# Moving the next batch's column norms and its query-weight product ahead of the output projection, in a two-layer post-norm kernel with five engines

## The chip, the cores and the metric

The kernel runs on one core of one Trainium2 chip. The metric is the device time of one execution in microseconds (us), the median of several runs. One further execution was recorded by the hardware profiler; all views of the profile and of the trace below belong to that one.

## What is computed

The input is 8 batches of 1024 tokens with 256 features. Two layers follow each other, each an attention-like step and a feed-forward step, and after each of the four steps the input is added back and a layer norm over the 256 features is taken. Cut to what matters here:

```python
# step 1: linear attention. Q, K, V = x @ W.T + b; Q and K are divided by their norms over the tokens
inv = 1.0 / jnp.linalg.norm(t, ord=2, axis=-2)
tailor_sum = 1.0 / (L + einsum('bnc,bc->bn', Q, sum(K, -1) + EPS))
matrix = einsum('bmn,bcn->bmc', K, V)
out = x + gamma * (value_sum + einsum('bnm,bmc->bcn', Q, matrix)) * tailor_sum
# step 2: 8 experts, all computed for every token, weighted with a thresholded softmax of x @ gate_w
# step 3: attention between the 16 heads of one token, then the output projection
out = einsum('bni,mi->bnm', attn @ v, Wproj) + bproj
# step 4: the best 768 of each 1024 tokens by a router score are replaced by gelu(x @ w_block)
```

The norms of step 1 are over tokens, so the kernel first makes the Gram matrix of a batch, multiplies it with the weights of Q and K, and gets the squared norms of all columns and the product with the query weights from that. These last two, called NORM and G, are what the change moves. The output projection of step 3 is called PR.

## The kernel before

**Stages.** The batches pass through a software pipeline written out by hand. In `turn(a, b, c)` batch a goes through step 1, batch b = a - 1 through step 2 and the projections to q, k and v, and batch c = a - 2 through steps 3 and 4. Turns are named by a here: turn 0 and turn 1 lack c (and b), turns 2 to 7 are full, then `closing` and `ending` finish the last two batches. Each engine has its own `turn` function, a fixed list of steps; an engine works its list strictly in order, and a step that waits for a semaphore holds everything behind it. So the written order is the schedule.

**Names.** `a_...` steps belong to batch a (also the expert steps `a_moe(b, t)`, t = 0 to 7, one for each 128 tokens; `ln(b, 4..7, 0)` is the norm after them), `b_...` steps to batch c (steps 3 and 4) or b. `TP` is 4: pairs of 128-token tiles. PSUM has eight banks: two for `a_` results, two for `b_` results, used in turn by the order of `A_USES` and `B_USES`, and four for the experts.

**Around the change**, in a full turn:

- TensorE (`pe`): `a_moe(b, 4)` (24 matmuls of 512 columns), `b_pr(c, 0..3)` (PR: 56 matmuls of 256 columns; it waits for `o_loaded`, the attention output of batch c, which is written to memory and read back in another layout by DMA: `scratch_o<-stage`, then `bt<-scratch_o`), `a_norm(a)` (NORM, 4 small fp32 matmuls, which show as 8 records; it waits for `t_sum`, from GpSimd), `a_g(a)` (G, fp32, 256 columns), `a_moe(b, 5)`, then `b_tz(c, 0..3)`, transposes of batch c's normalised rows `x3`.
- VectorE (`dve`): `a_moe(b, 4)`, `b_pr(c, p)` (add PR to `x3` at L1517, statistics at L1294 and L1299), `a_norm(a)` (copy the norms out of PSUM, L1326), `a_moe(b, 5)`, `b_tz(c, 0)` and `b_tz(c, 1)` (the low half of the split copy `ct`), `a_g(a)`.
- GpSimd (`pool`): `a_tsum(a)` (L632, L635, gives `t_sum`), `a_sum(b, 4)` (L619, L622, L626: adds ScalarE's expert parts), `ln(c, 0..3, 1)` (1/sqrt of the variance after PR), `a_norm(a)` (power -0.5 of the norms, L639).
- ScalarE (`act`), which the change doesn't touch: `a_moe(b, 4)`, `a_ln2n(b, 1)`, `b_prn(c, 0..3)` (normalises the rows after PR, L915, waits for `ln(c, p, 1)`), `a_moe(b, 5)` (four scaled copies out of expert banks 2 and 3, `part<-bank`), `b_tz(c, 0..3)` (the high half of `ct`, L794).

Two lines matter more than the others, since each stands at the head of a step that holds its engine:

```python
act.wait_ge(b_rs, 8 * b + p + 1)          # b_prn: ScalarE, ahead of its a_moe(b, 5)
pool.wait_ge(a_free[a_ring("NORM")], a_read(a, "NORM"))   # a_norm: GpSimd, waits for VectorE's copy
```

Of the kernel before, what the change touches and what calls it, by code (L numbers as in the profile page):

```python
# [5 lines left out]
def build_two_layer_postln(nc, x, wqk_t, bqk, wv, bv, gamma, gate_w, gate_b, expert_w, expert_b,  # L6
# [38 lines left out]
    with ctx:  # L45
# [200 lines left out]
        def a_ring(name):  # L246
            return a_use(name) % 2
# [14 lines left out]
        def a_read(a, name):  # L262
            return a * (UA // 2) + a_use(name) // 2 + 2
# [313 lines left out]
        def _(pool):  # L577
# [38 lines left out]
            def a_sum(a, t):  # L616

                pool.wait_ge(parted, T * a + t + 1)
                pool.tensor_tensor(part[:, 0:2, :], part[:, 0:2, :], part[:, 2:4, :], ALU.add)\  # L619
                    .then_inc(part_sum, 1)  # L620
                pool.wait_ge(part_sum, 2 * T * a + 2 * t + 1)
                pool.tensor_tensor(part[:, 0, :], part[:, 0, :], part[:, 1, :], ALU.add)\  # L622
                    .then_inc(part_sum, 1)
                pool.wait_ge(part_sum, 2 * T * a + 2 * t + 2)
                pool.wait_ge(chained, T * a + t + 1)
                pool.tensor_tensor(x1[:, t, :], x1[:, t, :], part[:, 0, :], ALU.add)\  # L626
                    .then_inc(moe_ready, 1)

            def a_tsum(a):
                pool.wait_ge(t_prod, 2 * a + 2)  # L630
                pool.sem_inc(waits_held, 1)
                pool.tensor_tensor(prod[:, 0, :], prod[:, 0, :], prod[:, 1, :], ALU.add).then_inc(t_sum, 1)  # L632
                pool.wait_ge(t_sum, 2 * a + 1)
                pool.wait_ge(t_row, a + 1)
                pool.tensor_tensor(prod[0:1, 0, :], prod[0:1, 0, :], prow, ALU.add).then_inc(t_sum, 1)  # L635

            def a_norm(a):
                pool.wait_ge(a_free[a_ring("NORM")], a_read(a, "NORM"))
                pool.tensor_tensor(inv[:, :], nrm[:, :], half[:, 0:4], ALU.pow).then_inc(inv_ready, 1)  # L639
# [29 lines left out]
            def turn(a, b, c):  # L669
                if b is not None:  # L670
                    a_sum(b, 0)
                    if c is not None:
                        b_turnv(c, 0)
                    a_sum(b, 1)
                if c is not None:
                    b_s(c, 0)
                    b_s(c, 1)
                    b_turnv(c, 1)
                if b is not None:
                    a_sum(b, 2)  # L680
                    ln(b, 4, 0)
                if c is not None:
                    b_s(c, 2)
                    b_s(c, 3)
                if b is not None:
                    a_sum(b, 3)
                    ln(b, 5, 0)
                if a is not None:
                    a_tsum(a)
                if b is not None:  # L690
                    a_sum(b, 4)
                if c is not None:
                    ln(c, 0, 1)
                    ln(c, 1, 1)
                    ln(c, 2, 1)
                    ln(c, 3, 1)
                if a is not None:
                    a_norm(a)
                if b is not None:
                    a_sum(b, 5)  # L700
                    ln(b, 6, 0)
                    a_sum(b, 6)
                    a_sum(b, 7)
                if c is not None:
                    ln(c, 4, 1)
                if b is not None:
                    ln(b, 7, 0)
                if c is not None:
                    ln(c, 5, 1)
                    b_store(c, 0)  # L710
                if a is not None:
                    ln(a, 0, 0)
                if c is not None:
                    b_store(c, 1)
                if b is not None:
                    b_copy(b, 0)
                if a is not None:
                    ln(a, 1, 0)
                if c is not None:
                    ln(c, 6, 1)  # L720
                if b is not None:
                    b_copy(b, 1)
                if c is not None:
                    ln(c, 7, 1)
                    b_store(c, 2)
                    b_store(c, 3)
                if b is not None:
                    b_copy(b, 2)
                if a is not None:
                    ln(a, 2, 0)  # L730
                if b is not None:
                    b_copy(b, 3)
                if a is not None:
                    ln(a, 3, 0)
                    if a + 1 < NB:
                        for p in range(TP):
                            a_xs(a + 1, p)
# [523 lines left out]
        def _(dve):  # L1261
# [62 lines left out]
            def a_norm(a):  # L1324
                dve.wait_ge(a_full, a_filled(a, "NORM"))
                dve.tensor_copy(nrm[:, :], a_ps("NORM")[:, 0:4]).then_inc(a_free[a_ring("NORM")], 1)  # L1326
# [100 lines left out]
            def a_moe(a, t):  # L1427
                dst = x1[:, t, :]
                if t % 2 == 0:
                    dve.wait_ge(a_free[a_ring(f"BIAS{t // 2}")], a_read(a, f"BIAS{t // 2}"))  # L1430
                for e in range(4):
                    q = e // 2
                    if e % 2 == 0:
                        dve.wait_ge(m_full, 32 * a + 4 * t + q + 1)
                    ins = dve.scalar_tensor_tensor(out=dst, in0=m_bank[q][:, D * (e % 2):D * (e % 2 + 1)],  # L1435
                                                   scalar=wexp[:, t, e:e + 1], in1=dst, op0=ALU.mult,
                                                   op1=ALU.add)
                    if e % 2 == 0:
                        ins.then_inc(m_step, 1)
                        dve.wait_ge(m_step, 2 * T * a + 2 * t + q + 1)  # L1440
                    else:
                        ins.then_inc(m_free[q], 1)
                        if q == 0:
                            dve.wait_ge(m_free[q], T * a + t + 2)
                dve.wait_ge(m_free[1], T * a + t + 2)
                dve.sem_inc(chained, 1)
# [152 lines left out]
            def turn(a, b, c):  # L1599
# [34 lines left out]
                    split_weights(range(0, 1))  # L1634
                if b is not None:
                    a_moe(b, 4)
                if c is not None:
                    for p in range(TP):
                        b_pr(c, p)
                if a is not None:  # L1640
                    a_norm(a)
                if b is not None:
                    a_moe(b, 5)
                if c is not None:
# [203 lines left out]
        def _(pe):  # L1848
# [49 lines left out]
            def a_norm(a):  # L1898
                pe.wait_ge(a_free[a_ring("NORM")], a_before(a, "NORM"))
                pe.wait_ge(t_sum, 2 * a + 2)  # L1900
                for c in range(4):
                    ins = pe.matmul(a_ps("NORM")[:, c:c + 1], prod[:, 0, P * c:P * (c + 1)], ones[:, 0:1],
                                    start=True, stop=True)
                ins.then_inc(a_full, 1)

            def a_g(a):
                pe.wait_ge(t_row, a + 1)
                pe.wait_ge(a_free[a_ring("G")], a_before(a, "G"))
                for m in range(KD):
                    cols = slice(D + P * m, D + P * (m + 1))  # L1910
                    ins = sum_of(a_ps("G")[:, D * m:D * (m + 1)],
                                 [(wqk[:, k, cols], tq[:, k, 0:D]) for k in range(KD)]
                                 + [(brow[0:1, cols], trow[0:1, 0:D])])
                ins.then_inc(a_full, 1)
# [63 lines left out]
            def a_moe(a, t, qs=range(4)):  # L1978
                for q in qs:
                    if t == 0 and later(a):  # L1980
                        pe.wait_ge(ff_read, 4 * (a - 1) + q + 1)
                    pe.wait_ge(m_free[q], T * a + t + 1)
                    sum_of(m_bank[q][:, :], split_terms(lambda k, i: at[:, k, i, tok(t)],
                                                        lambda k, j: we[:, j, k, 512 * q:512 * (q + 1)]))\
                        .then_inc(m_full, 1)
# [107 lines left out]
            def turn(a, b, c):  # L2093
# [31 lines left out]
                    a_tx(a, 1)  # L2125
                if b is not None:
                    a_moe(b, 4)
                if c is not None:
                    b_pr(c, 0)
                    b_pr(c, 1)  # L2130
                    b_pr(c, 2)
                    b_pr(c, 3)
                if a is not None:
                    a_norm(a)
                    a_g(a)
                if b is not None:
                    a_moe(b, 5)
                if c is not None:
# [220 lines left out]
```

## Time and profile before

| | us |
|---|---|
| median of 3 runs | 1359.78 (1359.39 to 1360.84) |
| profiled execution | 1357.91 |
| its span, first to last instruction | 1356.1 |
| mean granted TensorE clock, share of full speed | 0.886 |
| TensorE busy | 1167.6 (86%) |
| VectorE busy | 939.6 (69%) |
| ScalarE busy | 723.5 (53%) |
| GpSimd busy | 575.4 (42%) |

The profile's names are PE (TensorE matmuls), PEld (its weight loads), DVE (VectorE), ACT (ScalarE), POOL (GpSimd), SPq (the queue that issues most DMAs). A busy share is a mean over stages that have different limits, so what a change in one stage is worth must be read from the chain of waits in that stage. The profiled execution is 1.9 us below the median of the runs.

### The profile page before, as it was taken

The numbers are of one execution on the slowest core, as the hardware profiler recorded it, in microseconds if no ns is written. First come the engines' busy times: TensorE is split into PE (matmuls) and PEld (weight loads), VectorE is DVE, ScalarE is ACT, GpSimd is POOL, SyncE is SP. The second block draws the span as 40 slices with busy tenths as digits, with TensorE's granted clock in tenths as the row PEclk, the third lists the DMA queues.
The fourth block names the chain that finished last, engine by engine and source line by source line (L and its number), as shares of the span: only waits on it lengthen the run. The fifth ranks groups of instructions, "written<-read, shape, count | busy, mean of one in ns | idle before, by whom it ended". The sixth has DMA issues, their size and how long they took to land.

```text
span 1356.1 us, 31150 instructions
## 1 busy us (share of the span) xinstructions
PE 1167.6 (86%) x12264; PEld 749.5 (55%) x12264; DVE 939.6 (69%) x2118; ACT 723.5 (53%) x1152; POOL 575.4 (42%) x880
## 2 busy tenths in 40 slices
PE   6688899998989899998999989998999888996643
PEld 4444456655665546655665646555566555653532
DVE  3544578676766868677775868668776877656854
ACT  3223375347753575547853576447853566544444
POOL 2235335435354356345354355245354254350333
PEclk8789898799979997899979999799988998698566
DMA  5000092204802084202902065201902066108221
GB/s 187 16 1 16 31 154 21 80 9 113 114 3 78 19 173 44 79 9 92 135 2 79 17 164 56 56 24 61 170 6 64 1 138 81 38 27 156 33 79 47
DMA packets 93145, 90.64 MB, mean 67 GB/s; under 512 B 7110, under 2 KB 81864, under 8 KB 92744
## 3 DMA queue, kind: packets, MB, share of 16 engines
q1 hardware_dynamic: 80648, 75.54, 29.7%
q0 software_dynamic: 2560, 8.39, 1.8%
q10 hardware_dynamic: 9792, 4.72, 1.5%
q8 instruction: 98, 1.61, 0.5%
q14 instruction: 47, 0.39, 0.1%
HBM read 46.68 MB, written 41.94 MB: 65 GB/s over the span
## 4 chain that ended last, share of the span: by engine, by line
PE 55%; DVE 18%; DMA 6%; ACT 6%; issue 6%; POOL 6%; SPq 1%; ACTq 1%; POOLq 0%; DVEq 0%
PE bank L1852 52%; DVE keys L1546 2%; POOL rs L604 2%; DMA bt<-scratch_o 2%; DVE x L1435 2%; DVE stats L1294 2%; DVE gelu L1548 2%; DMA scratch_o<-stage 2%; PE bank L1862 2%; ACT x L915 1%; DVE ct L1263 1%; DVE gt L1349 1%; DVE x L1575 1%; ACT part L794 1%; ACT stage L794 1%
## 5 line engine op out<-in xcount | busy, mean ns | idle before, releaser
L1852 PE MATMUL bank<-we,at 128*128 128x512 f16 x1536 | 370.9, 400 | 1.9 <-DVE x L1435 1.9
L1852 PEld LDWEIGHTS bank<-we,at 128*128 128x128 f16 x1536 | 153.9, 102 | 192.4 <-issue 38.4
L619 POOL TENSOR_TENSOR part<-part 128x512 f32<-128x512 f32 x64 | 84.2, 1315 | 272.6 <-ACTq L941 272.6
L794 ACT ACTIVATE part<-bank,wexp 128x256 f32<-128x256 f32 x256 | 104.7, 472 | 160.3 <-PE bank L1852 99.7
L1435 DVE SCALAR_TENSOR_TENSOR x<-bank,wexp,x 128x256 f32<-128x256 f32 x256 | 122.7, 479 | 53.2 <-PE bank L1852 46.7
L1852 PE MATMUL bank<-bt,wqkv 128*128 128x512 f16 x576 | 137.1, 380 | 18.3 <-DVE stage L1263 12.3
L915 ACT ACTIVATE x<-x,nm,rs 128x256 f32<-128x256 f32 x192 | 104.5, 593 | 81.5 <-POOL nm L607 80.2
L1263 DVE TENSOR_TENSOR stage<-bank,stage 128x512 f16<-128x512 f32 x112 | 75.7, 686 | 86.5 <-ACT stage L794 86.2
L600 POOL TENSOR_SCALAR nm<-mv 128x2 f32<-128x2 f32 x128 | 33.6, 262 | 219.6 <-DVE mv L1299 213.9
L1852 PE MATMUL bank<-keys,blockdiag 128*128 128x16 f16 x3072 | 97.2, 193 | 22.1 <-DMA keys<-scratch_qkv 11.9
L1852 PEld LDWEIGHTS bank<-keys,blockdiag 128*128 128x128 f16 x3072 | 95.8, 103 | 26.9 <-issue 12.9
L794 ACT ACTIVATE stage<-bank 128x512 f16<-128x512 f32 x112 | 66.0, 597 | 80.0 <-PE bank L1852 74.5
L604 POOL TENSOR_TENSOR rs<-ve,half 128x2 f32<-128x2 f32 x128 | 96.0, 750 | 10.7
L1852 PEld LDWEIGHTS bank<-bt,wqkv 128*128 128x128 f16 x576 | 52.2, 98 | 83.8 <-DVE stage L1263 22.6
L1862 PE MATMUL bank<-const,x 128*128 128x128 f32 x384 | 59.8, 285 | 38.4 <-ACT x L915 24.0
L1852 PE MATMUL bank<-xs,blockdiag 128*128 128x16 f16 x2688 | 72.8, 172 | 16.9 <-issue 16.7
L1852 PEld LDWEIGHTS bank<-xs,blockdiag 128*128 128x128 f16 x2688 | 71.7, 101 | 19.0 <-issue 18.7
L794 ACT ACTIVATE blockdiag<-stage,const 128x2048 f16<-128x2048 f16 x40 | 78.1, 1994 | 1.5 <-DVE stage L1478 1.5
L1294 DVE BATCH_NORM_STATS2 stats<-x 128x6 f32<-128x256 f32 x192 | 71.9, 416 | 7.8 <-POOL x L626 4.1
L654 POOL COPY stage<-ct 128x2048 f16<-128x2048 f16 x14 | 53.3, 3810 | 56.2 <-DMA ct<-scratch_qkv 56.2
L1862 PEld LDWEIGHTS bank<-const,x 128*128 128x128 f32 x384 | 45.9, 146 | 53.9 <-ACT x L915 31.1
L1462 DVE TENSOR_SCALAR blockdiag<-stage,const 128x2048 f16<-128x2048 f16 x88 | 74.9, 902 | 0.0
(197 smaller groups left out, 2239.6 us busy)
## 6 DMA issues: line engine op xcount, KB each, us to landing
scratch_qkv<-stage SPq DMA_DIRECT2D x40, 512.0 KB, 3.5
ct<-scratch_qkv SPq DMA_DIRECT2D x112, 128.0 KB, 6.8
x_in<-in_x_dram SPq DMA_DIRECT2D x32, 256.0 KB, 2.8
keys<-scratch_qkv SPq DMA_DIRECT2D x64, 128.0 KB, 6.1
bt<-scratch_o SPq DMA_DIRECT2D x16, 512.0 KB, 4.1
out_dram<-x POOLq DMA_DIRECT2D x32, 256.0 KB, 2.6
scratch_qkv<-part SPq DMA_DIRECT2D x8, 512.0 KB, 8.1
scratch_o<-stage SPq DMA_DIRECT2D x32, 128.0 KB, 3.5
```

The source lines that it names most:

```text
L600: pool.tensor_scalar(nm[side][:, k, :], mv[side][:, k, :, 0], -1.0, None, ALU.mult)
L604: pool.tensor_tensor(rs[side][:, k, :], ve[side][:, k, :], half[:, 0:2], ALU.pow)\
L619: pool.tensor_tensor(part[:, 0:2, :], part[:, 0:2, :], part[:, 2:4, :], ALU.add)\
L654: pool.tensor_copy(v_rows[hf].rearrange("p (s c) h -> p s c h", c=8), turned(v_home(b), hf)).then_inc(v_turned[hf], 1)
L794: return act.activation(dst, src, ACT.Copy, scale=scale)
L915: ins = act.activation(dsts[t], srcs[t], ACT.Identity, bias=nm[side][:, k, t:t + 1], scale=rs[side][:, k, t:t + 1])
L1263: return dve.tensor_tensor(dst, src, hi, ALU.subtract)
L1294: ins = dve.bn_stats(stats[side][:, t, :], srcs[t])
L1435: ins = dve.scalar_tensor_tensor(out=dst, in0=m_bank[q][:, D * (e % 2):D * (e % 2 + 1)], scalar=wexp[:, t, e:e + 1], in1=dst, op0=ALU.mult ...
L1462: ins = dve.tensor_scalar(blockdiag[:, dst_half, :, DH * r:DH * (r + 1)], rows, mask[:, r:r + 1], None, ALU.mult)
L1852: ins = pe.matmul(dst, lhs, rhs, start=(n == 0), stop=(n == len(terms) - 1))
L1862: ins = pe.transpose(ps[:, 2 * P * k + P * t:2 * P * k + P * (t + 1)], src[:, 2 * p + t, P * k:P * (k + 1)], ident)
```

## The change

On TensorE `a_norm(a)` and `a_g(a)` go from behind the four `b_pr(c, p)` to ahead of them, right behind `a_moe(b, 4)`. On VectorE `a_norm(a)` goes ahead of `b_pr(c, p)`; `a_g(a)` stays. On GpSimd `a_norm(a)` goes ahead of `a_sum(b, 4)` and `ln(c, 0..3, 1)`, right behind `a_tsum(a)`. ScalarE and the DMA queues keep their lists. The order of use of the PSUM banks stays. Turns 2 to 7 change on all three engines, turn 1 on GpSimd alone.

```diff
@@ GpSimd, turn
                 if a is not None:
                     a_tsum(a)
+                if a is not None:
+                    a_norm(a)
                 if b is not None:
                     a_sum(b, 4)
                 if c is not None:
...
                     ln(c, 3, 1)
-                if a is not None:
-                    a_norm(a)
@@ VectorE, turn
                 if b is not None:
                     a_moe(b, 4)
+                if a is not None:
+                    a_norm(a)
                 if c is not None:
                     for p in range(TP):
                         b_pr(c, p)
-                if a is not None:
-                    a_norm(a)
@@ TensorE, turn
                 if b is not None:
                     a_moe(b, 4)
+                if a is not None:
+                    a_norm(a)
+                    a_g(a)
                 if c is not None:
                     b_pr(c, 0)
                     b_pr(c, 1)
                     b_pr(c, 2)
                     b_pr(c, 3)
-                if a is not None:
-                    a_norm(a)
-                    a_g(a)
```

TensorE in turn 2, before. `we` is the expert weight (so x24 is one `a_moe`), `wproj` and `bproj` are PR, `ones,shared` is NORM, `wqk` and `brow` are G:

```order
L1852 MATMUL bank<-we,at 128x512 x24
L1852 MATMUL bank<-wproj,bt 128x256 x6
L1852 MATMUL bank<-bproj,rows 128x256
...
L1902 MATMUL bank<-ones,shared 128x1 x4
L1852 MATMUL bank<-xs,wqk 128x256 x2
L1852 MATMUL bank<-xs,brow 128x256
...
L1852 MATMUL bank<-we,at 128x512 x24
L1862 MATMUL bank<-const,x 128x128 x16
```

And with the change:

```order
L1852 MATMUL bank<-we,at 128x512 x24
L1902 MATMUL bank<-ones,shared 128x1 x4
L1852 MATMUL bank<-xs,wqk 128x256 x2
L1852 MATMUL bank<-xs,brow 128x256
...
L1852 MATMUL bank<-wproj,bt 128x256 x6
L1852 MATMUL bank<-bproj,rows 128x256
...
L1852 MATMUL bank<-we,at 128x512 x24
L1862 MATMUL bank<-const,x 128x128 x16
```

NORM and G now stand between one expert step and PR; PR stands directly ahead of the next expert step. What follows, the transposes (`const,x`), is where it was.

GpSimd in turn 2, before. `shared` is `a_tsum`, `part` and `x` are `a_sum`, `nm`, `ve`, `rs` one `ln`, `inv` is `a_norm`:

```order
L632 TENSOR_TENSOR shared<-shared 128x512
L635 TENSOR_TENSOR shared<-shared,xs 1x512
L619 TENSOR_TENSOR part<-part 128x512
...
L626 TENSOR_TENSOR x<-x,part 128x256
L600 TENSOR_SCALAR nm<-mv 128x2
...
L607 TENSOR_TENSOR nm<-nm,rs 128x2
L639 TENSOR_TENSOR inv<-nrm,half 128x4
```

And with the change:

```order
L632 TENSOR_TENSOR shared<-shared 128x512
L635 TENSOR_TENSOR shared<-shared,xs 1x512
L639 TENSOR_TENSOR inv<-nrm,half 128x4
L619 TENSOR_TENSOR part<-part 128x512
...
L626 TENSOR_TENSOR x<-x,part 128x256
L600 TENSOR_SCALAR nm<-mv 128x2
...
L607 TENSOR_TENSOR nm<-nm,rs 128x2
```

The power of the norms moved past one `a_sum` and four `ln` steps.

## Rows read from the trace of the kernel before

**Rows 1.** Page, section 4: engines' shares of the chain that ended last.

```profile
PE 55%; DVE 18%; DMA 6%; ACT 6%; issue 6%; POOL 6%; SPq 1%; ACTq 1%; POOLq 0%; DVEq 0%
```

**Rows 2.** Chain of waits, turn 5: start us, us, engine, tile, line.

```profile
727.85 6.29 PE bank L1852 x56
...
744.49 0.61 ACT ct L794
```

**Rows 3.** Timeline of TensorE, turn 4: start us, us, operation, [idle before <-releaser].

```profile
567.64 5.34 PE L1852 MATMUL bank<-we,at 128*128 128x512 f16 x24
572.82 0.82 PE L1852 MATMUL bank<-wproj,bt 128*128 128x256 f16 x6
...
578.94 0.95 PE L1902 MATMUL bank<-ones,shared 128*128 128x1 f32 x8
...
583.10 5.35 PE L1852 MATMUL bank<-we,at 128*128 128x512 f16 x24
588.29 1.04 PE L1862 MATMUL bank<-const,x 128*128 128x128 f32 x8
590.92 1.22 PE L1862 MATMUL bank<-const,x 128*128 128x128 f32 x8 [1.59 <-DVE ct L1263]
```

**Rows 4.** Timeline of TensorE, turns 2, 5 and 6, ahead of PR.

```profile
262.46 0.83 PE L1852 MATMUL bank<-wproj,bt 128*128 128x256 f16 x6 [0.77 <-DMA bt<-scratch_o]
...
721.24 5.34 PE L1852 MATMUL bank<-we,at 128*128 128x512 f16 x24
727.85 0.83 PE L1852 MATMUL bank<-wproj,bt 128*128 128x256 f16 x6 [1.27 <-DMA bt<-scratch_o]
...
883.32 0.83 PE L1852 MATMUL bank<-wproj,bt 128*128 128x256 f16 x6 [0.40 <-DMA bt<-scratch_o]
```

**Rows 5.** Timeline of ScalarE, turns 4 and 5.

```profile
583.57 1.09 ACT L915 ACTIVATE x<-x,nm,rs 128x256 f32<-128x256 f32 x2 [0.57 <-POOL nm L607]
587.25 0.84 ACT L794 ACTIVATE part<-bank,wexp 128x256 f32<-128x256 f32 x2 [2.59 <-issue]
588.49 0.84 ACT L794 ACTIVATE part<-bank,wexp 128x256 f32<-128x256 f32 x2 [0.41 <-PE bank L1852]
589.45 1.09 ACT L794 ACTIVATE ct<-bank 128x512 f16<-128x512 f32 x2
...
738.54 1.09 ACT L915 ACTIVATE x<-x,nm,rs 128x256 f32<-128x256 f32 x2 [0.67 <-POOL nm L607]
```

**Rows 6.** Timeline of ScalarE, an expert step whose four copies ran back to back.

```profile
705.25 1.57 ACT L794 ACTIVATE part<-bank,wexp 128x256 f32<-128x256 f32 x4
```

**Rows 7.** Timelines of TensorE and VectorE in turn 1, which has no PR.

```profile
122.08 1.01 PE L1902 MATMUL bank<-ones,shared 128*128 128x1 f32 x8
...
126.31 5.35 PE L1852 MATMUL bank<-we,at 128*128 128x512 f16 x24
...
123.13 0.16 DVE L1326 COPY nrm<-bank 128x4 f32<-128x4 f32 x1 [2.07 <-PE bank L1902]
```

**Rows 8.** Timeline of GpSimd, turn 4.

```profile
571.40 1.26 POOL L635 TENSOR_TENSOR shared<-shared,xs 1x512 f32<-1x512 f32 x1
573.99 1.28 POOL L619 TENSOR_TENSOR part<-part 128x512 f32<-128x512 f32 x1 [1.33 <-ACTq L941]
```

**Rows 9.** View of line L639: duration ns min/median/max, first and last start us.

```profile
L639 POOL TENSOR_TENSOR inv<-nrm,half x8: 1007/1014/1041, 32.6 to 1047.7; 128x4 f32<-128x4 f32 x8
```

**Rows 10.** Timeline of TensorE: `a_moe(b, 1)` of turn 3, `a_moe(b, 4)` of turn 3, `a_moe(b, 1)` of turn 5.

```profile
358.54 5.34 PE L1852 MATMUL bank<-we,at 128*128 128x512 f16 x24
...
413.82 5.34 PE L1852 MATMUL bank<-we,at 128*128 128x512 f16 x24
...
667.66 5.34 PE L1852 MATMUL bank<-we,at 128*128 128x512 f16 x24
```

**Rows 11.** Windows: span, length, five engines' busy time (instructions), TensorE clock, DMA share, GB/s.

```profile
554.00:562.00 8.00, 7.16 (x198) 6.68 (x199) 4.79 (x9) 2.29 (x5) 2.08 (x3) 0.50 0.02 4
566.00:618.00 52.00, 48.83 (x311) 29.92 (x309) 38.82 (x109) 22.64 (x45) 23.55 (x39) 1.00 0.13 43
```

## The prediction

> **What bounds the kernel now.** I read the page's chain first: TensorE holds 55% of it, but VectorE, ScalarE, GpSimd and DMA hold the rest [rows 1]. So the end is set by a chain that changes engines, and I have to ask which engine ends last in the stage of the change. The chain of waits of turn 5 answers: it is on TensorE through PR, NORM, G and `a_moe(b, 5)`, then it leaves TensorE for two things on ScalarE, the last copies of that expert step and the first `ct` copy, [rows 2], and the transposes behind wait for VectorE's half of that copy [rows 3]. The same order stands in turns 2 to 7. The event to watch is therefore the start of that `ct` copy. Whatever moves it moves all that comes after.
>
> I measure from M, the moment at which TensorE is through with `a_moe(b, 4)`. In turn 4 that step starts at 567.64 and PR follows without idle time at 572.82, so one expert step takes 5.18 and M = 572.82. NORM starts at 578.94 (PR took 6.12), `a_moe(b, 5)` at 583.10 (NORM and G took 4.16), the transposes at 588.29 (5.19) [rows 3]. ScalarE's last two copies start at 588.49 and the `ct` copy at 589.45 [rows 5], 1.16 after the expert step. Sum: M + 6.12 + 4.16 + 5.19 + 1.16 = M + 16.63. In turns 3, 4 and 7 TensorE has no idle time ahead of PR. In turns 2, 5 and 6 it waits for the DMA that brings `bt`, and everything is later by that wait, w. The row of turn 5 says 1.27, counted from the modelled end of the last matmul; counted from M = 721.24 + 5.18 = 726.42 it is 1.43 [rows 4]. The same 0.16 added to the idle of 0.77 and 0.40 in turns 2 and 6 gives 0.93 and 0.56 [rows 4]. **Before: `ct` copy at M + 16.63 + w, with w adding up to 2.92 over six turns.** As a cross-check, turn 5 gives 726.42 + 1.43 + 16.63 = 744.48, and the chain has 744.49 [rows 2].
>
> **What the change does on TensorE.** NORM and G fill the wait: PR can start at M + 4.16 and `bt` came at M + 1.43 at the latest, so w is gone in all turns. No work is added. NORM must not wait itself: it needs GpSimd's second sum, which ends at 571.40 + 1.26 = 572.66, 0.16 ahead of M [rows 8]. That is narrow, but turn 1 already runs the new order, since it has no PR: NORM starts at 122.08 and the next expert step at 126.31, 4.23 in all against 4.16 [rows 7]. I take 4.23. If TensorE alone set the end, the gain would be 2.92 less six times 0.07.
>
> **What it does on the way through PR.** PR now starts later by 4.23 - w. Behind PR hangs a chain on other engines: VectorE's addition and statistics, GpSimd's four `ln`, ScalarE's four normalisations. From the start of PR at 727.85 [rows 4] to the end of the last normalisation, 738.54 + 1.09 = 739.63 [rows 5], it takes 11.78 when nothing else holds it. In turn 4 it is a little shorter in tail, but there its first `ln` was held by `a_sum` on GpSimd (572.82 to 583.57 + 1.09 = 584.66 is 11.84) [rows 3, 5]. So 11.78 it is: **after, the normalisations end at M + 4.23 + 11.78 = M + 16.01.**
>
> **Where they collide.** On ScalarE's list `b_prn` stands ahead of `a_moe(b, 5)`, whose copies free expert banks and come ahead of `ct`. Before, ScalarE was through with the normalisations at 584.66 and stood idle 2.59 until TensorE had filled the bank at 587.25 [rows 5]. That idle time is the only slack. After, the bank is full at the same distance from M, 587.25 - 572.82 = 14.43, plus the 0.07 of NORM, so at M + 14.50; but ScalarE is free only at M + 16.01. The four copies then run back to back, 1.57 [rows 6] in place of 2.09 with a gap, and end at M + 17.60 with 0.02 to start; from their end to the `ct` copy it is 589.45 - (588.49 + 0.84) = 0.12 [rows 5]. **After: `ct` copy at M + 17.72, whatever w is.** The difference in one turn is 17.72 - 16.63 - w = 1.09 - w.
>
> **The sum.** Six turns: 6 x 1.09 - 2.92 = +3.6 us. By turn it is +0.2, +1.1, +1.1, -0.3, +0.5, +1.1. The ends of the uncertain terms: if the four copies keep 2 x 0.84 = 1.68 it is 0.11 more a turn (+4.3); if NORM and G take 4.16 it is 0.07 less (+3.2). The profiled execution would go from 1357.91 to 1361.5; the median stands 1.87 above the profiled one, and 1359.78 + 3.6 = 1363.4.
>
> **Edits at no cost, and their cover.** VectorE's copy of the norms comes 1.05 after NORM starts and takes 0.16 (123.13 against 122.08) [rows 7]; in its new place VectorE would be waiting for PR anyway until M + 4.23. If NORM were late, VectorE would hold PR's additions, but those need TensorE, which would be held too. GpSimd waits for that copy: norms at M + 1.21, the power takes 1.01 [rows 9], then `a_sum(b, 4)`, three additions of which the first and widest takes 1.28 [rows 8], so 3.9 at most: it ends by M + 6.1. ScalarE reads it in the copies of `a_moe(b, 5)`, at M + 16. Behind it on GpSimd stands the first `ln`, which can't have its statistics before PR has started at M + 4.23 and VectorE has added and measured a pair; if this cover were short by x, the PR chain would be longer by x. In turn 1 the sum ends by 123.29 + 1.01 + 3.9 = 128.2, and its reader waits for the third of four banks of the expert step that starts at 126.31 [rows 7], so for 130.2; I cost it at nothing. VectorE's share of `a_moe(b, 5)` stands behind the statistics of PR, which feed the last normalisations and so end before M + 15; ScalarE's share ends later than its own.
>
> **A rule against the sum.** The row shows 1.27 of TensorE idle for a DMA in turn 5 [rows 4]. The Trainium skill, page Perfetto Trace Analysis, section Optimization Strategies, says that the goal in general is to keep the matmul engine as busy as possible. By that rule filling these idle times is the gain, and it is my second rival. The trace speaks against it here, as ScalarE's slack of 2.59 is smaller than the 4.23 by which PR moves.
>
> **Rivals.**
> 1. *TensorE keeps the end* (faster). ScalarE's normalisations would have to end before the bank is full, at M + 14.50 instead of M + 16.01. The point from which this decides is a PR chain of 10.27 or less in place of 11.78. Then each turn changes by 0.07 - w: 0.4 - 2.9 = -2.5, or 1357.3; with NORM and G at 4.16, 1356.9. For it: TensorE is 55% of the chain. Against: rows 5.
> 2. *The delay is swallowed* (same). The chain shows only the last releaser, and another path might be so near that the local loss of turns 3, 4 and 7 doesn't arrive, or half of it does: 0 to +1.8, so 1359.8 to 1361.6. Against: between the `ct` copy and the next turn the chain is VectorE almost without idle time.
> 3. *The clock changes sides* (much slower, or no loss). The stage of the change runs at a granted 1.00, which is 2.4 GHz, and the attention stage of 16-column matmuls ends at 0.50, which is 1.2 GHz [rows 11]. The expert steps between the attention steps fall into slow or fast stretches as it happens. From `a_moe(b, 1)` to M it took 413.82 + 5.18 - 358.54 = 60.46 in turn 3 and 726.42 - 667.66 = 58.76 in turn 5 [rows 4, 10], for the same instructions. The shift of each turn moves these stretches. Turns 3 and 6 are of the long kind, the others short; three short ones turned long cost 5.1 (1368.5), two long ones turned short give back 3.4 (1360.0).
> 4. *NORM waits.* If GpSimd's sums came after M, TensorE would stand still with PR behind it. Cover 0.16; each 0.5 us late would cost 3.0 over six turns. Turn 1 speaks against it. It is in the range with the third.
>
> **Chances.** Forecast (1362 to 1365): 0.50. TensorE keeps the end: 0.10. Swallowed: 0.15. Clock or NORM, upward: 0.20; clock downward: 0.05. The range leaves out the first rival and takes in the clock's ends: 1359.6 to 1368.0. A measurement tells this kernel from no change from about 0.2%, 2.7 us, so slower means over 1362.5. Of the forecast's 0.50 some 0.40 lies above it, and 0.20 of the third rival; of TensorE's 0.10 some 0.07 is below 1357.1. Slower 0.60, within 0.32, faster 0.08.
>
> **What would show each step.** No idle time ahead of PR in any turn, and NORM at M without a wait. ScalarE's last normalisation ending at M + 16.0, and its four expert copies back to back (1.57) in all six turns, released by ScalarE itself and not by TensorE. The `ct` copy at M + 17.7. TensorE idle for VectorE's `ct` about 1.1 longer than the 1.59 of turn 4 [rows 3], or 2.7. I am wrong if that idle stays at 1.59, if ScalarE still waits for the bank, or if the stretches from `a_moe(b, 1)` to M add up to several us more or less than before.

## The result, and the profile after

The changed kernel takes 1366.80 us (median of 5 runs, 1365.55 to 1367.82), the kernel before 1359.78. The ratio is 1.0055, 95% interval 1.0037 to 1.0072: by the ratio 7.5 us slower, between 5.0 and 9.8 (the two medians are 7.0 apart). The profiled execution took 1365.55, against 1357.91 before, 7.6 more.

TensorE first, turn 4 (timeline: start, duration, operation, idle time before it and what ended it):

```profile
567.46 5.34 PE L1852 MATMUL bank<-we,at 128*128 128x512 f16 x24
572.64 0.99 PE L1902 MATMUL bank<-ones,shared 128*128 128x1 f32 x8
...
582.97 5.34 PE L1852 MATMUL bank<-we,at 128*128 128x512 f16 x24
588.15 1.04 PE L1862 MATMUL bank<-const,x 128*128 128x128 f32 x8
591.66 1.23 PE L1862 MATMUL bank<-const,x 128*128 128x128 f32 x8 [2.47 <-DVE ct L1263]
592.72 0.66 PE L1919 MATMUL bank<-shared,ones 128*128 128x256 f32 x2
593.38 2.07 PE L1852 MATMUL bank<-shared,ones 128*128 128x256 f32 x4
595.38 1.22 PE L1852 MATMUL bank<-xs,rowtmp 1*128 1x256 f32 x2
596.53 4.43 PE L1852 MATMUL bank<-ct,wrt 128*128 128x512 f16 x12
```

NORM starts at 572.64, right at M (567.46 + 5.18), so it doesn't wait, and the next expert step starts 10.33 after M against 10.28 in [rows 3]. The waits of [rows 4] are gone in all six turns. But the idle time for `ct`, 1.59 in [rows 3], is 2.47. And look at the last four lines. They are IQCS (small fp32 products of batch a, the lines with `shared,ones` and `xs,rowtmp`) and the router product of batch c (`ct,wrt`), and their lengths in a turn without trouble are these, from turn 5 of the same kernel:

```profile
751.17 1.23 PE L1862 MATMUL bank<-const,x 128*128 128x128 f32 x8 [2.48 <-DVE ct L1263]
752.23 0.60 PE L1919 MATMUL bank<-shared,ones 128*128 128x256 f32 x2
752.89 1.13 PE L1852 MATMUL bank<-shared,ones 128*128 128x256 f32 x4
753.95 0.69 PE L1852 MATMUL bank<-xs,rowtmp 1*128 1x256 f32 x2
754.57 2.76 PE L1852 MATMUL bank<-ct,wrt 128*128 128x512 f16 x12
```

2.07 against 1.13, 4.43 against 2.76. The windows of turn 4 say why (columns as in [rows 11]; the clock is the third number from the end): the granted clock is 1.00 through the idle time, as in [rows 11], and 0.50 behind it, that is 1.2 in place of 2.4 GHz. Read in narrower windows, it falls about 1.5 us after TensorE has started again, at 593.2, and is back at 1.00 at 600.0.

```profile
586.00:590.00 4.00, 3.19 (x19) 1.81 (x17) 1.54 (x4) 3.34 (x8) 1.28 (x4) 1.00 0.00 0
590.00:594.00 4.00, 2.34 (x12) 1.64 (x13) 3.18 (x8) 2.35 (x5) 2.77 (x3) 0.89 0.00 0
594.00:598.00 4.00, 4.00 (x10) 1.72 (x9) 2.34 (x7) 0.39 (x1) 1.81 (x4) 0.50 0.00 0
```

In the kernel before the same window has 1.00:

```profile
594.00:598.00 4.00, 3.55 (x21) 1.58 (x19) 3.74 (x9) 1.86 (x4) 1.90 (x4) 1.00 0.00 0
```

Such a fall stands in turns 4 and 6 of the changed kernel's profile, and in no turn of before. From the `ct` copy to `a_moe(b, 6)` it is 10.55 in the turns without it, in both kernels, and 13.69 in the two with it: TensorE is 3.14 later each time. The chain that ends last feels a little less of it. In a turn without a fall it runs over VectorE there, and reaches VectorE's first `keys` step (L1546) 9.87 behind the `ct` copy; in turn 4 it runs over TensorE's slow steps and reaches it 12.35 behind, 2.48 later. From the chain of waits, turns 4 and 5:

```profile
590.19 0.61 ACT ct L794
...
593.38 7.61 PE bank L1852 x18
...
602.54 1.12 DVE keys L1546 x2
...
749.70 0.61 ACT ct L794
...
759.57 1.12 DVE keys L1546 x2
```

ScalarE in turn 4, beside [rows 5]:

```profile
582.27 1.09 ACT L915 ACTIVATE x<-x,nm,rs 128x256 f32<-128x256 f32 x2 [7.39 <-POOL nm L607]
...
587.54 1.09 ACT L915 ACTIVATE x<-x,nm,rs 128x256 f32<-128x256 f32 x2 [0.66 <-POOL nm L607]
588.53 1.54 ACT L794 ACTIVATE part<-bank,wexp 128x256 f32<-128x256 f32 x4
590.19 1.08 ACT L794 ACTIVATE ct<-bank 128x512 f16<-128x512 f32 x2
```

The 2.59 of slack (idle time that could be used up without harm) ahead of the expert copies is gone; they run back to back behind the last normalisation, released by nothing but ScalarE's own list, and the `ct` copy is at 590.19 = M + 17.55, where it was at M + 16.63. In all six turns it is between M + 17.55 and M + 17.58. The chain of waits, which in [rows 2] ran over TensorE from PR to the expert step, now leaves it inside PR and comes to ScalarE's copies over VectorE and GpSimd (turn 5):

```profile
733.14 4.93 PE bank L1852 x26
738.09 0.70 DVE x L1517
738.82 0.77 DVE stats L1294 x2
...
746.02 0.72 POOL rs L604
746.81 0.21 POOL nm L607
...
747.55 0.59 ACT x L915
748.13 1.46 ACT part L794 x4
...
749.70 0.61 ACT ct L794
```

**The account of the two profiles.** The `ct` copies of the six turns stand at 105.4 us behind their M in sum, against 102.7: +2.7. Two falls of the clock: +6.3. That makes +9.0, where the two profiles differ by 7.6. The rest, -1.3, is +1.0 in the stretches from `a_moe(b, 6)` to the next M and -2.4 behind the last turn.

This account is made of two single executions, and the stretches between the turns vary by more than its rest. One kernel of the next section was profiled twice, as `e6_late_norm_in_before` and `e10_late_norm_in_before_again`. The six stretches from `a_moe(b, 1)` to M, which the prediction's third rival is about, add up to 355.0 in one and 360.4 in the other; they are 357.3 in before and 357.8 in the changed kernel. In the changed kernel's profile the stretches behind the two falls are of the long kind, 60.57 in turn 5 and 60.58 in turn 7, where before has 58.76 and 58.84. Whether a fall brings that along or it is chance isn't shown.

### The profile page after: what moved, and what is told of

Read it like the earlier page. It is cut to its first block, busy times and chain, and to the rows that moved or that the text cites. A ratio compares the mean times of both kernels' runs of the same rounds, so it can differ in the third digit from the quotient of the medians.

```text
span 1363.8 us, 31150 instructions
## 1 busy us (share of the span) xinstructions
PE 1171.8 (86%) x12264; PEld 749.9 (55%) x12264; DVE 938.6 (69%) x2118; ACT 721.8 (53%) x1152; POOL 573.6 (42%) x880
## 4 chain that ended last, share of the span: by engine, by line
PE 54%; DVE 18%; POOL 8%; issue 7%; ACT 7%; DMA 4%; SPq 1%; ACTq 0%; POOLq 0%; DVEq 0%
PE bank L1852 51%; POOL rs L604 3%; DVE keys L1546 2%; DVE stats L1294 2%; PE bank L1862 2%; DVE gelu L1548 2%; DVE x L1435 2%; ACT x L915 2%; ACT part L794 1%; POOL nm L607 1%; DVE x L1575 1%; POOL ve L601 1%; POOL nm L600 1%; DVE ct L1263 1%; DMA out_dram<-x 1%
## 5 line engine op out<-in xcount | busy, mean ns | idle before, releaser
L794 ACT ACTIVATE at<-bank 128x512 f16<-128x512 f32 x64 | 38.2, 596 | 62.8 <-PE bank L1862 61.2
```

What stands on the lines that cost most here:

```text
L794: return act.activation(dst, src, ACT.Copy, scale=scale)
```

## The experiments

The ratios are against the kernel before on the same chip. Where marks are given, M is TensorE's end of `a_moe(b, 4)`, as in the prediction, and they were read in all six full turns of each profile. On the chips of these experiments single executions of the kernel before ran from 1349.5 to 1366.7 us, so only medians of many are compared, and a single profile can't price a change of a few us.

**ScalarE's hold taken away.** In the changed kernel:

```diff
                     b_prn(c, 2)
-                    b_prn(c, 3)
                 if b is not None:
                     a_moe(b, 5)
                 if c is not None:
                     b_tz(c, 0)
                     b_tz(c, 1)
+                    b_prn(c, 3)
                     b_tz(c, 2)
```

> The changed kernel, and on ScalarE the fourth normalisation after PR goes behind the second ct copy, so that the copies of a_moe(b, 5) no longer stand behind the whole PR chain. Two theories of where the 7 us of the change come from. Theory A: on ScalarE the PR chain (M + 16.0) holds the expert copies and with them the ct copy by about 0.95 us a turn, less the filled wait, 2.7 us over six turns; and the idle time of TensorE for ct, which this lengthens from 1.59 to 2.48, makes the granted clock fall to 0.50 behind it in some turns (two of six in the profile, 3.1 us each). It expects the ct copy at M + 16.7, the idle at 1.59, no stretch at 0.50 between a_moe(b, 5) and a_moe(b, 6), and the three filled waits as gain: 2.5 us faster than before, ratio 0.998. Theory B: ScalarE's order costs nothing, the 7 us come from the attention stage, whose slow stretches fall otherwise after a shift of TensorE's work: it expects about 1.005 here too.

Measured: 0.9965 (0.9946 to 0.9985), 4.8 us faster than before. ScalarE waits for TensorE's bank again, and the `ct` copy is at M + 16.67 or 16.68 in all turns. Turn 4:

```profile
583.51 1.09 ACT L915 ACTIVATE x<-x,nm,rs 128x256 f32<-128x256 f32 x2 [0.66 <-POOL nm L607]
584.83 0.84 ACT L794 ACTIVATE part<-bank,wexp 128x256 f32<-128x256 f32 x2 [0.23 <-issue]
586.08 0.84 ACT L794 ACTIVATE part<-bank,wexp 128x256 f32<-128x256 f32 x2 [0.41 <-PE bank L1852]
587.04 1.09 ACT L794 ACTIVATE ct<-bank 128x512 f16<-128x512 f32 x2
588.01 1.08 ACT L915 ACTIVATE x<-x,nm,rs 128x256 f32<-128x256 f32 x2
```

TensorE's idle time for `ct` is back at 1.59 (third transpose step at 588.50), and no turn has a fall of the clock there. Theory B, that the attention stage makes the whole loss whatever ScalarE does, is out: the shift of TensorE's work is the same here and the loss is gone. That the attention stage has a microsecond or two in it isn't excluded, since the later `ct` copy shifts it too. This kernel beats both.

**NORM alone ahead.** In the changed kernel `a_g(a)` goes back behind the four `b_pr(c, p)`:

```diff
                     a_norm(a)
-                    a_g(a)
                 if c is not None:
                     b_pr(c, 0)
...
                     b_pr(c, 3)
+                if a is not None:
+                    a_g(a)
```

> The changed kernel with G back behind PR: NORM alone (0.87 us) stands ahead of PR. Theory A: PR starts at M + 0.87, or when bt is there; the PR chain ends at M + 12.7, inside ScalarE's slack of 2.6, so the ct copy is at M + 16.7; of the waits up to 0.87 is filled: about 2 us faster than before, ratio 0.9985, and no stretch at 0.50 after a_moe(b, 5). Theory B, that any shift of TensorE's work ahead of PR brings the loss through the attention stage: slower than before by several us, 1.003 to 1.006.

Measured: 0.9982 (0.9964 to 0.9999), 2.4 us faster. ScalarE keeps 1.44 of slack (turn 4) where it had 2.59, and the `ct` copy is at M + 16.58 to 16.77 in five turns and 17.23 in the one where `bt` came 1.49 after M. No fall of the clock. So a small shift of PR is free. That fits a loss which begins where ScalarE's slack ends, but between shifts of 0.87 and 4.22 no kernel was run.

**TensorE's idle time filled, the delay kept.** In the changed kernel five unused matmuls:

```diff
+            def filler(a):
+                pe.wait_ge(a_free[a_ring("IQCS")], a_before(a, "IQCS"))
+                for _ in range(5):
+                    pe.matmul(a_ps("IQCS"), rows16[:, :], we[:, 0, 0, 0:512], start=True, stop=True)
...
                     b_tz(c, 1)
+                    filler(a)
                     b_tz(c, 2)
```

> The changed kernel with five unused matmuls of 512 columns (5 x 0.22 = 1.1 us) on TensorE between the second and the third transpose step, inside its idle time of 2.48 for ct; they write a PSUM bank that IQCS overwrites, and wait for nothing new. Theory A: ScalarE's delay stays (ct copy at M + 17.6), but the idle time is back to 1.4 and the granted clock doesn't fall behind it: 2.7 us slower than before, ratio 1.002. Theory B, that the idle time has nothing to do with it: no change from the changed kernel, 1.0055.

Measured: 1.0020 (1.0003 to 1.0037), 2.7 us slower than before (0.4 to 5.0), as theory A had it. The `ct` copy stays at M + 17.6; the idle time is 1.39, and the same steps that took 2.07 and 4.43 take 1.13 and 2.76, in this and in all other turns:

```profile
588.60 1.04 PE L1862 MATMUL bank<-const,x 128*128 128x128 f32 x8
589.47 1.24 PE L1919 MATMUL bank<-we,rows 128*128 128x512 f16 x5
592.11 1.23 PE L1862 MATMUL bank<-const,x 128*128 128x128 f32 x8 [1.39 <-DVE ct L1263]
593.17 0.60 PE L1924 MATMUL bank<-shared,ones 128*128 128x256 f32 x2
593.83 1.13 PE L1852 MATMUL bank<-shared,ones 128*128 128x256 f32 x4
...
595.52 2.76 PE L1852 MATMUL bank<-ct,wrt 128*128 128x512 f16 x12
```

Work that does nothing gave back some 4.8 us of the 7.5. The changed kernel wasn't run on this chip, but its three measurements (1.0055, and 1.0072 and 1.0062 below) lie above this one (the interval of the first just touches this one's, those of the others don't). This separates the two parts of the loss: ScalarE's delay, some 2.7, and the clock behind TensorE's idle time. And the delay isn't swallowed further on: `e1_norm_late`, the same chip and a `ct` copy 0.89 earlier in each turn, is 7.6 us faster than this kernel, where six times 0.89 is 5.3.

**The delay by itself.** In the kernel before, on ScalarE between `a_moe(b, 5)` and `b_tz(c, 0)`:

```diff
+                    for n in range(3):
+                        copy(iq[:, 64 * n:64 * (n + 1)], const[:, 0:64])
                     b_tz(c, 0)
```

> The kernel before, and on ScalarE three small copies into an unused stretch of iq ahead of the first ct copy, about 1.0 us: it prices the delay of the ct copy by itself, with PR, NORM and G where they were. Theory A: each of six turns is 1.0 longer (6 us), and as TensorE's idle time is then 2.6, the clock falls behind it in some turns, 3.1 us each: 9 to 18 us slower, ratio 1.007 to 1.013. If the delay counts but the clock isn't tied to the idle time: 6 us, 1.0045. If the delay is swallowed further on: under 1.002.

Measured: 1.0072 (1.0046 to 1.0099), 9.8 us slower. The dose was smaller than meant: three small copies take 0.45, not 1.0. What comes behind is another 0.35 later, as two steps of VectorE ahead of IQCS take 0.88 there in place of 0.51; why isn't known. TensorE's idle time rose to 2.02, and the clock fell behind it in three of six turns, in two of them for half as long as in the changed kernel (0.9 to 1.0 us lost each, 3.0 in the third). Six times 0.8 and 4.9 is 9.7, well inside the interval of 6.2 to 13.4.

**The same with the full dose**, eight copies of 32 columns in place of three:

```diff
-                    for n in range(3):
-                        copy(iq[:, 64 * n:64 * (n + 1)], const[:, 0:64])
+                    for n in range(8):
+                        copy(iq[:, 32 * n:32 * (n + 1)], const[:, 0:32])
```

> The kernel before with eight small copies on ScalarE ahead of the first ct copy in place of e4_ct_delay's three, some 1 us, so that TensorE's idle time for ct is 2.5 to 2.6, as in the changed kernel, or above. It prices the changed kernel's idle time with PR, NORM and G untouched. Theory A: 0.9 to 1.3 us for each of six turns (5.4 to 7.8), and in two to four turns a fall of the granted clock behind the idle time, 3.1 each: 12 to 20 us slower, ratio 1.009 to 1.015. If the fall in the changed kernel needed the moved PR: 6 to 8 us, 1.0045 to 1.006, and no stretch at 0.50 there.

Measured: 1.0086 (1.0064 to 1.0108), 11.7 us slower, just under the 12 to 20 that was expected; the delay of the `ct` copy is 0.97, the idle time 2.54. Three of six turns have the fall, which by the marks cost 3.2, 1.4 and 3.0; with 6 x 0.97 that is 13.4, inside the interval (8.7 to 14.7). Turn 2:

```profile
279.31 1.04 PE L1864 MATMUL bank<-const,x 128*128 128x128 f32 x8
282.88 1.22 PE L1864 MATMUL bank<-const,x 128*128 128x128 f32 x8 [2.54 <-DVE ct L1265]
283.94 0.61 PE L1921 MATMUL bank<-shared,ones 128*128 128x256 f32 x2
284.56 2.08 PE L1854 MATMUL bank<-shared,ones 128*128 128x256 f32 x4
```

PR, NORM and G are where they were in these two kernels, so the fall comes with the longer idle time and doesn't need the moved work.

**GpSimd's part undone**, its list as before, the rest changed:

```diff
                 if a is not None:
                     a_tsum(a)
-                if a is not None:
-                    a_norm(a)
...
                     ln(c, 3, 1)
+                if a is not None:
+                    a_norm(a)
```

> The changed kernel with GpSimd's list as it was: the power of the norms behind a_sum(b, 4) and the four ln. Theory A (ScalarE's order and the clock): GpSimd has no part in the loss, its list has idle time on both sides: ratio as the changed kernel, 1.0055, ct copy at M + 17.6. If GpSimd's wait for VectorE's copy of the norms held the ln of the PR chain, this would give back up to 1 us a turn: ct copy at M + 16.6 and about 1.001.

Measured: 1.0072 (1.0056 to 1.0088). Nothing comes back; `ct` copy at M + 17.6, two falls of the clock, in turns 3 and 7. GpSimd's edit costs nothing that can be seen beside the changed kernel's 1.0062 on the same chip, as forecast.

**The changed kernel again.**

> The changed kernel once more, for a second profile of it and on the same chip as these. Theory A: ct copy at M + 17.6 in all turns again; a stretch at 0.50 behind the idle time of 2.5 in some turns, not necessarily in the same ones (one to four of six); ratio 1.004 to 1.007. If the stretches of the first profile were a single event, none.

Measured: 1.0062 (1.0046 to 1.0078). `ct` copy at M + 17.55 or 17.56; one fall, in turn 4, behind an idle time of 2.47 like that of the other turns. In three profiles with this idle time and PR moved, the fall stands in 2, 2 and 1 turns of six. In five profiles with an idle time of 1.59 or less, and two repetitions below, it stands in none.

**ScalarE's edit alone, in the kernel before.** The diff is that of the first experiment.

> The kernel before with ScalarE's edit of e1_norm_late alone: the fourth normalisation goes behind the second ct copy. Theory A: in the order of before ScalarE has 2.6 us of slack, so this does nothing: ct copy at M + 16.6 + w, ratio 1.000, and the gain of e1_norm_late (0.9965) comes from the filled waits for bt, which need NORM and G ahead. If ScalarE's edit gains by itself: 0.997.

Measured: 0.9985 (0.9966 to 1.0003), which decides nothing between 1.000 and 0.997. The marks say that nothing moved: the slack of ScalarE is larger, the `ct` copy at M + 16.62 + the wait. So both kernels were run again side by side.

> The kernel of e1_norm_late once more, beside the next run on the same chip, since the intervals of e1_norm_late and e6_late_norm_in_before overlap. With the waits filled and ScalarE's hold gone: 2.5 us faster than before by the marks of the trace, 0.998; a second value near 0.9965 would mean 2 us more that the marks don't explain.

> The kernel of e6_late_norm_in_before once more, beside e9: ScalarE's edit alone, expected at 1.000 (its ct copy is at M + 16.6 + w as before). If ScalarE's edit gains by itself, both this run and e9 are lower by the same amount.

Measured: 0.9969 (0.9949 to 0.9989) with NORM and G ahead, 1.0002 (0.9980 to 1.0023) without. The gain needs both edits, though the intervals of these last two overlap. It is 4.2 to 4.8 us where the marks of the first profile of before give 2.7. Part of that is the wait itself, which varies from execution to execution: in sum over six turns it was 2.9 in the first profile, 2.6 and 4.6 in those of ScalarE's edit alone, 4.7 and 2.7 in the two with the delay. Their mean of 3.5 gives a gain of 3.2, 0.9976, inside both intervals; whether a microsecond or so is left over, from the attention stage for one, these runs can't tell.

## Why the prediction was right, and where it was not

The forecast was slower by 3.6 us, 1363.4; it is 7.5 slower, 1366.8, inside the range but above the 1362 to 1365 that had the chance of 0.50. It falls in the part of the range that was there for the third rival, the clock, and that rival stood for another place. So the direction and the delay on ScalarE were foreseen, and that the range reached far enough is in part luck.

*TensorE.* Right. PR starts at M + 4.21 to 4.23 (4.23 was taken), NORM never waits, the 0.16 of cover held in all turns. The waits for `bt` are filled.

*The collision on ScalarE.* Right in place and mechanism, and nearly in size. Normalisations end at M + 16.0 as computed; the copies take 1.54 in place of 1.57 and begin 0.1 before the last normalisation is written, so the `ct` copy is at M + 17.57, not 17.72. The term is 0.94 - w for a turn where 1.09 - w stood, and the sum +2.7 where +3.6 stood. `e3_filled_gap` measured it by itself: 2.7, with an interval of 0.4 to 5.0, so that the two figures are the same is luck. With w at 3.5, its mean over five profiles, the sum would be 2.1.

*The rule against the sum.* The Trainium skill, page Perfetto Trace Analysis, section Optimization Strategies, wants the matmul engine kept busy. The change filled 2.9 us of idle time ahead of PR and lost; with ScalarE's hold removed the same filled waits gained 4 to 5 us. The rule isn't contradicted: what was filled ahead of PR came back behind it, as 0.88 more idle time for `ct` in each of six turns, 5.3 in all. In this kernel the filled time is a gain only where the engine held behind it has slack for the move. The prediction calls this rule its second rival; by its list it is the first, TensorE keeps the end.

*The cover on GpSimd and VectorE.* Right: GpSimd's list could be put back with no change in time. VectorE's edit wasn't undone by itself, but in the trace its first addition comes 1.73 behind the start of PR in turn 4 of before and of the changed kernel, so nothing held it.

*The clock.* This is the step that failed: the sum had no term for it. The prediction priced the clock in the third rival, as stretches of the attention stage that fall otherwise, up to +5.1, and set the stage of the change itself at 1.00 throughout. It named the longer idle time for `ct` as a mark to look for, and gave it no price beyond its own length. The runs showed the price: behind an idle time of 2.5 the clock fell in some turns, 3.1 us each, 5 of 18 turns in the three profiles with the moved PR, so some 5 us for an execution by TensorE's marks, 4 by the 2.5 that the chain showed. That this is near the rival's 5.1 is a coincidence; the place was wrong, and it should have been a term of the sum. What the rival did describe hardly moved in the two profiles: its own sign, the sum of the stretches from `a_moe(b, 1)` to M, went from 357.3 to 357.8, with turns 5 and 7 turned long and turn 6 short. It was also misread in part: turn 2 of before is long as well, with 60.24, so three turns were long and not two, and its upper end, 1368.5, lies above the range that was said to take it in. The Trainium skill, page TensorE: Matmul & The Clock Gate, section What's actually happening, has the array's clock set by how busy it has been lately. The trace agrees as far as it goes: in turn 4 it is 1.00 ahead of the idle time of 2.47 and 0.50 from 1.5 us behind its end.

*The other rivals.* TensorE keeping the end is out in this kernel, but it is what `e1_norm_late` made true. That the delay is swallowed is out: two kernels on one chip whose `ct` copies stand 5.3 us apart over six turns were 7.6 apart. NORM never waited.

## What to carry to other kernels

Before filling an idle time of one engine with work from behind, ask which chain starts at the step that is pushed back, and on which in-order list its end stands ahead of something that is on the critical path; the slack there (2.6 us here) against the push (4.2 less the wait) decided it here. If it is short, look for the one step that can go behind the critical one: here a single line on ScalarE turned a loss of 7.5 us into a gain of 4.2 to 4.8. And an idle time on TensorE that grows by 1 us in an otherwise busy stage can cost some 3 us more in a turn, since what comes behind it may run at half the clock; here that came in 5 of 18 turns.

## What the runs showed of the hardware

- The granted clock fell to 0.50 behind a single idle time of 2.5 us, in a stage where TensorE was busy on both sides: in 8 of 24 turns with 2.46 to 2.54 (the changed kernel twice, GpSimd's part undone, the full dose of delay), in 3 of 6 with 2.02, and in none of 36 with 1.59 or of 6 with 1.39. In 8 of these 11 it stayed at 0.50 for 6.6 to 7.0 us, in the other three for about half of that. What decides whether a given turn has it, the runs don't show; the turns differ from execution to execution.
- Small copies on ScalarE overlap: one of 64 columns lasts 0.24 in `e4_ct_delay`, but three took only 0.45 to the start of the next copy, 0.15 each, and eight of 32 columns in `e7_more_ct_delay` 0.97, 0.12 each.
- The wait for a DMA on the critical path isn't one number: its sum over six turns was 2.6 to 4.7 us in five profiles of kernels with the same order there.
